# Two graph layers on one core: r transposed in 32x32 blocks through memory, W2 a graph later, row statistics on ScalarE, and the attention's result ahead of the next logits' maximum

## The reference, cut to what matters

```
# layer 0: attention with 8 heads of 64 units
feats  = h @ W[head];  e_self = feats @ a_self;  e_neigh = feats @ a_neigh
att    = softmax(leaky_relu(e_self[i] + e_neigh[j], 0.2) masked by adj)
x      = x + relu(att @ feats + b)
# layer 1: two hypergraph convolutions (H = adj != 0, w = first row of adj)
conv(v, W, b) = Dn * (H @ (Be * (H^T @ (v @ W^T)))) + b
r      = relu(conv(h, W1, b1))                    # 128 x 1024
y      = conv(layer_norm(r) * gamma + beta, W2, b2)
out    = y + h + x
```

## Time and profile before

| | |
|---|---|
| median of 3 runs | 2591.59 us |
| profiled execution, its own time | 2593.87 us |
| its span (first to last instruction) | 2591.9 us |
| TensorE busy | 2527.3 us, 98% |
| VectorE busy | 1968.6 us, 76% |
| GpSimd busy | 1630.6 us, 63% |
| ScalarE busy | 1423.3 us, 55% |
| mean granted TensorE clock | 0.993 of full speed |
| DMA queue of SyncE | 105456 packets, 201.60 MB |

### The profile page before, as it was taken

How to read it: one execution, slowest core, us unless ns; L and a number is a source line. 1 busy time by engine, 2 the same in 40 slices (tenths; PEclk the granted TensorE clock), 3 DMA queues, 4 the chain that set the end, 5 groups by cost and what they waited for, 6 DMA issues and landing times.

```text
span 2591.9 us, 50876 instructions
## 1 busy us (share of the span) xinstructions
PE 2527.3 (98%) x14996; PEld 2195.1 (85%) x14996; DVE 1968.6 (76%) x4640; ACT 1423.3 (55%) x3465; POOL 1630.6 (63%) x2068
## 2 busy tenths in 40 slices
PE   3899999999999999999999999999999999999998
PEld 2788888888888888888888888888888888888886
DVE  5877777777777777777777777777777777777774
ACT  2555555555555555555555555555555555555553
POOL 4666666666666666666666666666666666666663
PEclk8899999999999999999999999999999999999999
DMA  5122222222222222222222222222222222222210
GB/s 183 63 75 80 77 76 80 74 79 77 73 79 74 80 79 74 80 76 77 77 73 79 74 80 79 74 80 79 74 80 72 82 79 71 79 75 80 79 65 26
DMA packets 105480, 201.89 MB, mean 78 GB/s; under 512 B 20080, under 2 KB 36464, under 8 KB 105456
## 3 DMA queue, kind: packets, MB, share of 16 engines
q1 hardware_dynamic: 105456, 201.60, 23.5%
HBM read 167.39 MB, written 34.15 MB: 78 GB/s over the span
## 4 chain that ended last, share of the span: by engine, by line
PE 85%; DVE 8%; issue 3%; POOL 2%; DMA 1%; ACT 1%; SPq 0%; POOLq 0%; DVEq 0%
PE p_w1a L843 12%; PE p_w1a L839 12%; PE p_w1a L838 12%; PE p_att L917 7%; PE p_w1b L953 5%; PE p_w1b L839 5%; PE p_w1b L843 5%; PE p_w1b L838 5%; PE p_att L897 4%; PE p_fa L834 2%; PE p_fa L832 2%; PE p_fa L833 2%; PE p_fb L832 2%; PE p_fb L833 2%; PE p_fb L834 2%
## 5 line engine op out<-in xcount | busy, mean ns | idle before, releaser
L392 POOL TENSOR_TENSOR rs<-ve,halfpow 128x1 f32<-128x1 f32 x128 | 117.8, 921 | 544.8 <-DVE ve L774 544.8
L380 POOL TENSOR_TENSOR u<-u,mask 128x1024 f32<-128x1024 f32 x128 | 306.3, 2393 | 182.0 <-DMA u<-en_rows 182.0
L838 PE MATMUL p_w1a<-W_hi,rT_hi 128*128 128x512 f32 x1024 | 415.5, 406 | 0.0
L457 ACT ACTIVATE att<-u,shifts 128x128 f32<-128x128 f32 x1024 | 400.5, 391 | 18.4 <-DVE shifts L734 10.5
L839 PE MATMUL p_w1a<-W_lo,rT_hi 128*128 128x512 f32 x1024 | 404.1, 395 | 0.0
L458 ACT ACTIVATE att_low<-u,shifts 128x128 f32<-128x128 f32 x1024 | 399.5, 390 | 0.0
L843 PE MATMUL p_w1a<-W_hi,rT_lo 128*128 128x512 f32 x1024 | 280.8, 396 | 0.0
L502 ACT ACTIVATE rT_hi<-p_tb 128x512 fp32r<-128x512 f32 x128 | 76.6, 598 | 333.5 <-PE p_tb L864 333.5
L917 PE MATMUL p_att<-feats,attT 128*128 128x65 f32 x2048 | 242.9, 272 | 2.2 <-ACT attT L492 2.2
L917 PEld LDWEIGHTS p_att<-feats,attT 128*128 128x128 f32 x2048 | 239.6, 192 | 2.7 <-ACT attT L492 2.7
L789 DVE SCALAR_TENSOR_TENSOR raw<-p_w1a,rs,t_bc 128x512 f32<-128x512 f32 x128 | 96.1, 750 | 187.2 <-PE p_w1a L843 187.2
(11 more groups left out here) (125 smaller groups left out, 7216.9 us busy)
## 6 DMA issues: line engine op xcount, KB each, us to landing
u<-en_rows SPq DMA_DIRECT2D x130, 576.0 KB, 3.6
x_in<-in_x SPq DMA_DIRECT2D x128, 256.0 KB, 2.6
xT_in<-in_xT SPq DMA_DIRECT2D x128, 256.0 KB, 3.2
out<-raw SPq DMA_DIRECT2D x128, 256.0 KB, 2.0
adj_in<-in_adj SPq DMA_DIRECT2D x128, 128.0 KB, 2.5
en_rows<-eT SPq DMA_DIRECT2D x520, 1.1 KB
raw<-in_W1T SPq DMA_DIRECT2D x2, 1024.0 KB, 8.1
raw<-in_W2T SPq DMA_DIRECT2D x2, 1024.0 KB, 9.7
```

The source lines that it names most:

```text
L380: nc.gpsimd.tensor_tensor(u[:, g.slot(2), 0:HEADS, :], u[:, g.slot(2), 0:HEADS, :], mask[:, :].unsqueeze(1).broadcast_to([P, HEADS, N]), A ...
L392: nc.gpsimd.tensor_tensor(rs1[:, :], ve1[:, :], halfpow[:, :], ALU.pow).then_inc(s_rs1, 1)
L457: nc.scalar.activation(att[:, i, :], u[:, g.slot(2), i, :], ACT.Exp, bias=shifts[:, 0, i:i + 1])
L838: mm(dst, hi, w_hi, start=first, stop=False)
```

## The change

r's transposition leaves TensorE. VectorE transposes r (128 x 1024) within 32x32 blocks into rB, SyncE writes rB to a scratch in memory (`r_blocks`) and, once it has landed, reads it back by four DMAs that put the blocks in their places in rT, in runs of 32 values (128 bytes). ScalarE then makes rT_hi at the end of its turn in one instruction, VectorE rT_lo at the beginning of the next turn in one instruction.

The product with W2 is that of graph t-1, and z and y and the output are one graph later with it. There is one turn more (t up to 129). `rest` has four buffers in place of two, `rs2` two columns in place of one.

The two `bn_stats` and the `bn_aggr` over r are gone from VectorE. The two ReLUs on ScalarE also sum their rows (`accum_out`), two small instructions make the negative mean, one `Square` over 1024 columns sums the squared deviations, and another small one makes the variance; GpSimd keeps the root alone.

On ScalarE the first ReLU of r stands ahead of h0's high part, and z's high part ahead of hg's. On VectorE sizes, counts and reciprocals stand ahead of r's second half; and the maximum of the logits of t+2 with what follows it stands behind x1's statistics of t+1. The load of x of t+5 is issued by ScalarE, that of adj at the beginning of SyncE's turn.

```diff
 # turns
-    loops = (total - AHEAD - 2) // UNROLL
-    for t in range(-AHEAD, 1):
+    loops = (total - AHEAD - 3) // UNROLL
+    for t in range(-AHEAD, 2):
...
 # SyncE
+                if t.plus(5).within(NG) and (t.loop is not None or t.base >= -1):
+                    load_adj(t.plus(5))
...
-                g = t.plus(5)
-                if g.within(NG) and (g.loop is not None or g.base >= 4):
-                    load(g)
+                g = t
+                if g.within(NG):
+                    sp.wait_ge(s_rB, g.count())
+                    sp.dma_start(r_blocks[:, :], rB).then_inc(s_rB_out, 16)
+                    sp.wait_ge(s_rB_out, g.count(per=16))
+                    for c in range(4):
+                        sp.dma_start(rT[32 * c:32 * (c + 1), :].rearrange("a (k q b) -> a k q b", q=4, b=32),
+                                     r_blocks.rearrange("(q a) (k c b) -> c a k q b", q=4, c=4, b=32)[c]).then_inc(s_rT, 16)
...
 # ScalarE, in the order of its turn
                     exps(t.plus(1), 1)
+                nc.scalar.activation(r[:, 0:HALF], r[:, 0:HALF], ACT.Relu, accum_out=sum2[:, 0:1]).then_inc(s_r, 1)
                 ... h0's high part
-                ... ReLU of r's first half, rT_hi's first half
+                nc.scalar.activation(nm2a[:, :], sum2[:, 0:1], ACT.Copy, scale=-1.0 / DH).then_inc(s_nm2a, 1)
                 act.wait_ge(s_pre, g.count(per=2))
+                nc.scalar.activation(r[:, HALF:DH], r[:, HALF:DH], ACT.Relu, accum_out=sum2[:, 1:2]).then_inc(s_r, 1)
                 ... copy of the transposed attention weights of t+1
-                ... rT_hi's second half
+                nc.scalar.activation(nm2[:, :], sum2[:, 1:2], ACT.Identity, bias=nm2a[:, :], scale=-1.0 / DH).then_inc(s_nm2, 1)
+                nc.scalar.activation(dev, r, ACT.Square, bias=nm2[:, :], accum_out=sq2[:, :]).then_inc(s_sq2, 1)
                 ... G's high part (of t-1)
+                nc.scalar.activation(ve2[:, :], sq2[:, :], ACT.Identity, bias=eps[:, :], scale=1.0 / DH).then_inc(s_ve2, 1)
                     exps(t.plus(2), 0)
+                    act.wait_ge(s_x1, g.count(4))
+                    act.dma_start(x_in[:, g.slot(4), :], x[bass.ds(n, 1), :, :].rearrange("a p d -> p (a d)")).then_inc(s_in[g.slot(4)], 16)
                 ... h of t+1
+                ... z's high part of t-1, ahead of hg's high part
                 ... hg's high part of t+1
+                    act.wait_ge(s_rT, g.count(per=64))
+                    nc.scalar.activation(rT_hi[:, :], rT, ACT.Copy).then_inc(s_rT_hi, 1)
                 ... copy of G of t+2
...
 # VectorE, in the order of its turn
                     feats_of(g, 1, scale)
+                g = t.plus(-1)
+                    dve.wait_ge(s_rT_hi, g.count())
+                    nc.vector.tensor_tensor(rT_lo[:, :], rT, rT_hi[:, :], ALU.subtract).then_inc(s_rT_lo, 1)
                 ... r's first half, larger(t+1, 1), h0's low part, incidence of t+2
+                ... sizes, counts, reciprocals of t+2
                 ... r's second half
-                ... sizes, bn_stats
                 ... y (of t-2)
-                ... rT_lo's first half, bn_stats, counts, reciprocals, bn_aggr
-                ... maximum of the logits of t+2, neg_s, neg_m, shifts
+                    dve.wait_ge(s_r, g.count(per=2))
+                    nc.vector.transpose(rB, r[:, :]).then_inc(s_rB, 1)
                 ... rden, o_sc of t+1
-                ... rT_lo's second half
                 ... x1, bn_stats, inv, bn_aggr, ve1, nm1 of t+1
+                ... maximum of the logits of t+2, neg_s, neg_m, shifts
+                        dve.wait_ge(s_rs1, t.plus(1).count())
                     larger(t.plus(2), 0)
                 ... z (of t-1), statistics of t+5, hg's low part
...
 # TensorE
-                    transposes(p_ta, r[:, 0:HALF], s_rT)
-                    transposes(p_tb, r[:, HALF:DH], s_rT)
                 ... the last product is that of t-2, the product with W2 that of t-1
+                    pe.wait_ge(s_rT_hi, g.count())
+                    if t.within(NG):
+                        pe.wait_ge(s_pre, t.count(per=2) - 1)
+                    for c in range(HC):
+                        high(p_w1a[:, :], rT_hi[:, part(c)], W2_hi[:, c, :], W2_lo[:, c, :], c == 0)
+                    pe.wait_ge(s_rT_lo, g.count())
+                    for c in range(HC):
+                        last = low(p_w1a[:, :], rT_lo[:, part(c)], W2_hi[:, c, :], c == HC - 1)
```

More of the change, by code:

```diff
@@ L58, in turns @@
     with eng.Fori(0, loops) as k:
[L59 removed]
+        for u in range(2, UNROLL + 2):
             turn(Graph(u, k))
[L61 removed]
+    for t in range(2 + loops * UNROLL, total + 2):
         turn(Graph(t))
@@ L520, in turn @@
                         rounded(3)
+                g = t.plus(-1)
+                if g.within(NG):
+                    act.wait_ge(s_z, g.count())
+                    if g.has(1):
+                        act.wait_ge(s_y, g.count(1))
+                    nc.scalar.activation(z_hi[:, :], z[:, :], ACT.Copy).then_inc(s_z_hi, 1)
                 g = t.plus(1)
@@ L736, in turn @@
+                g = t
+                if g.within(NG):
+                    dve.wait_ge(s_r, g.count(per=2))
+                    if g.has(1):
+                        dve.wait_ge(s_rB_out, g.count(1, per=16))
+                    nc.vector.transpose(rB, r[:, :]).then_inc(s_rB, 1)
+                if t.base == -1:
+                    rest_of(2)
+                if t.base == -2:
+                    rest_of(1)
+                g = t.plus(2)
                 g = t.plus(1)
@@ L746, in turn @@
                                             ALU.mult).then_inc(s_osc, 1)
-                if t.within(NG):
-                    dve.wait_ge(s_rT_hi, t.count(per=2))
-                    nc.vector.tensor_tensor(rT_lo[:, HALF:DH], p_tb[:, :], rT_hi[:, HALF:DH],
-                                            ALU.subtract).then_inc(s_rT_lo, 1)
                 if g.within(NG):
@@ L921, in turn @@
                     spread()
-                g = t
+                g = t.plus(-1)
                 if g.within(NG):
-                    pe.wait_ge(s_r, g.count(per=2))
-                    if g.has(1):
-                        pe.wait_ge(s_y_sb, g.count(1))
-                    if g.plus(1).within(NG):
-                        pe.wait_ge(s_G_sb, g.plus(1).count())
-                    transposes(p_tb, r[:, HALF:DH], s_rT)
-                    for m in range(2):
-                        if g.base == 0:
-                            pe.wait_ge(k_lo2, 1 + m)
-                        pe.wait_ge(s_rT_hi, g.count(per=2) - 1 + m)
-                        for c in range(m * CB, (m + 1) * CB):
-                            high(p_w1a[:, :], rT_hi[:, part(c)], W2_hi[:, c, :], W2_lo[:, c, :], c == 0)
-                        pe.wait_ge(s_rT_lo, g.count(per=2) - 1 + m)
-                        for c in range(m * CB, (m + 1) * CB):
-                            last = low(p_w1a[:, :], rT_lo[:, part(c)], W2_hi[:, c, :], c == HC - 1)
+                    pe.wait_ge(s_rT_hi, g.count())
+                    if t.within(NG):
+                        pe.wait_ge(s_pre, t.count(per=2) - 1)
+                    for c in range(HC):
+                        if g.base == 0 and c % CB == 0:
+                            pe.wait_ge(k_lo2, 1 + c // CB)
+                        high(p_w1a[:, :], rT_hi[:, part(c)], W2_hi[:, c, :], W2_lo[:, c, :], c == 0)
+                    pe.wait_ge(s_rT_lo, g.count())
+                    for c in range(HC):
+                        last = low(p_w1a[:, :], rT_lo[:, part(c)], W2_hi[:, c, :], c == HC - 1)
                     last.then_inc(s_w2, 1)
@@ L969, in turn @@
                         pe.wait_ge(s_G_sb, g.count(1))
+                    if g.has(4):
+                        pe.wait_ge(s_y_sb, g.count(4))
                     mm(p_G, inc[:, g.slot(2), 1, :], beT[:, :], start=True, stop=True).then_inc(s_G, 1)
```

186 lines of the change are left out of this document (91 added, 95 removed).

## The result

The changed kernel takes 3074.91 us (median of 4 runs, 3065.77 to 3100.26), the kernel before 2590.73 beside it: a ratio of 1.188, with an interval of 1.184 to 1.193. It is 484 us slower. The forecast was 2920 us with a range of 2780 to 3100. The profiled execution took 3100.26 us, the longest of the four, its span 3098.3, at a mean granted clock of 0.916; the kernel before had 0.993.

The account below looks back on a forecast made before the run. TensorE's own work was taken to bound the 19.51 us turn. Turn 18.63 + 0.82 + 2.19 + 0.47 = 22.11 us, 325 us over 125 turns; 2593.87 + 325 + 11 - 10 = 2920 us, range 2780 to 3100.

Parts of the forecast that it names:

- third case: Rival: r's way through memory decides the turn; at 40 ns a packet the ring takes 25.6 us, 3357 us in all; chance 0.14.
- The product of h for h: TensorE waits for h, queued on ScalarE behind exponentials that wait for the late shifts: 8.16 - 5.97 = 2.19 us a turn.
- The attention's product for attT: TensorE waits for ScalarE's copy of the transposed attention weights, behind r's late second half and its ReLU: 0.82 us a turn.
- second case: Rival: only h is late, VectorE getting r's second half out in time; turn 21.02 us, 2784 us in all; chance 0.10.
- The restarts: TensorE's products behind the two waits take longer, 1.17 against 0.97 and 2.00 against 1.73: 0.47 us a turn.
- The clock stays: TensorE's granted clock remains 1.00 despite the waits, from a stretch with 4.31 of 5 us busy; no time added.
- 11 at the end less 10 in the first turns: 11 us more for the last graph's r through memory, 10 less because setup stalls can hide the new waits.
- The way through memory: r's write of 512 KB within 3.6 us, reads with landing 7.4, over before ScalarE comes to rT_hi: costs nothing.
- the end of like size: Lower of two prices for the reads' 128-byte packets, 21 ns against 92, from packets of the same size: 5.4 us.
- the ring: Way through memory, then rT_hi, copy of G and exponentials, to the next turn's ReLU: 20.8 us, less than the forecast turn.
- Hidden costs: VectorE's block transposition and rT_lo, some 1.2 us each, and ScalarE's statistics fit into idle time; rT_lo up to 0.3 short.
- Case 4: Rival: faster, the transposes' removal from TensorE worth 0.88 x 125 = 110 us, less 11 at the end: 2495 us; chance 0.07.

Follow-up runs that it names:

- e1: Changed kernel with VectorE's maximum of the next logits, up to the shifts, put back ahead of the attention's result: 2599.95 us, ratio 1.003 to the kernel before.
- e6: Kernel before the change with only VectorE's maximum of the logits of t+2, up to the shifts, moved behind x1's statistics of t+1: 3080.37 us, ratio 1.188.
- e10: Changed kernel, maximum still late, with exps(t+2, 0) moved from ahead of h to ScalarE's turn end and larger(t+2, 0) a turn later: 3262.48 us, ratio 1.257.
- e4: Changed kernel with unread TensorE products added, 3 ahead of the wait for attT and 8 ahead of the wait for h: 2881.39 us, ratio 1.111.
- e7: e1 with r's blocks read from memory twice, by four more DMAs, and rT_hi waiting for all eight: 3075.5 us, ratio 1.187 to the kernel before.
- e5: e1 with two parts of the features of t+3 moved on TensorE to ahead of the attention's product: 2601.43 us, ratio 1.003 to the kernel before.
- e2: Changed kernel with r's second half ahead of sizes and counts on VectorE, h0's high part ahead of r's first ReLU on ScalarE: 2874.05 us, ratio 1.108.
- e8: e1 with h0's high part put back ahead of r's first ReLU on ScalarE: 2566.22 us, ratio 0.990 to the kernel before.

## Why the prediction was right, and where it was not

**The time.** The measured 3074.91 us lie above the forecast's own range, 2814 to 3029. They lie within the stated range only because its upper end was widened for the mild part of the third case, the way through memory, which had no part in it. That the range holds is luck; that the kernel became slower, and by which two waits, is not.

**The product of h for h: right, by its steps.** In the turn from 1074.78 the way runs as worked out. Changed kernel, VectorE, then ScalarE:

```profile
1076.81 0.21 DVE L768 RECIPROCAL rden<-p_att 128x8 f32<-128x8 f32 x1 [1.64 <-PE p_att L952]
1079.76 1.21 DVE L803 TENSOR_REDUCE neg_max<-u 128x8 f32<-128x1024 f32 x1
1081.42 0.17 DVE L812 TENSOR_TENSOR shifts<-e_blk,neg_m 128x16 f32<-128x16 f32 x1
```

```profile
1081.71 0.40 ACT L474 ACTIVATE att<-u,shifts 128x128 f32<-128x128 f32 x1 [5.15 <-DVE shifts L812]
1082.07 0.34 ACTq L549 DMA_DIRECT2D x_in<-in_x  x1
...
1084.06 0.80 ACT L558 ACTIVATE h<-x,nb,rs 128x512 f32<-128x512 f32 x1
```

From the product's end (1074.78 + 2.00) to the product of h (1084.99) it is 8.21 us; 8.16 were forecast, and the wait was 2.17 where 2.19 stood. The load of x on ScalarE goes out between exponentials and costs nothing; 0.10 had been taken. e1 takes the cause away and the wait goes, e6 makes it alone and the wait comes, e10 moves the exponentials alone and the wait goes.

**The attention's product for attT: there, but of two kinds.** Forecast 0.82 us. In most turns shown it is 0.26 to 0.57, because the counts take 0.17 and not the 0.39 of the earlier trace rows, and a row sum adds about 0.10 to a ReLU in place of 0.14. In the others it is 2.0 to 2.5: there the counts last 1.9 to 2.4 us beside GpSimd's addition, in 32 of 129 executions, or the incidence 2.5, in three. Together 0.96 a turn; that this is near 0.82 is luck. The had the sign of it: 0.39 us for two columns is long, and the prediction saw that (in its second case) but took it only as something that could shrink.

**The restarts: right where the clock held.** The products behind the two waits take 1.15 and 2.00 us, as in the earlier trace rows.

**"The clock stays": the step that failed.** It was put at nothing, from a single row of the last turns at 4.31 of 5 us busy and 1.00. The runs showed that in the changed kernel, behind a single wait of 2.0 to 2.5 us, the clock mostly falls to 0.50 for some microseconds, and e4 that it stays when the waits are filled. That row, with 0.69 us idle in all, held no wait of that length. The price stands in the window of the main part, 122 turns:

```profile
135.82:3008.56 2872.74, 2537.95 (x13298) 2180.84 (x13299) 1978.05 (x4025) 1544.26 (x4027) 1552.90 (x1828) 0.92 0.39 109
```

TensorE is busy 2537.95 / 122 = 20.80 us a turn, against 19.14 in the turn at full clock: 1.66 us a turn, 203 us in 122 turns. With this term the sum closes: 18.63 + 0.96 + 1.85 + 0.47 + 1.66 = 23.57 us a turn, against 2872.74 / 122 = 23.55 measured; 125 x (23.57 - 19.51) = 508 us, against 3100.26 - 2593.87 = 506 in the two profiled executions. The forecast's 11 at the end less 10 in the first turns was not tried.

**The way through memory: rightly given no part in this kernel, but for a reason that is half luck.** The write lands in 2.6 us (at most 3.6 forecast), and the four reads go out in 2.8 to 2.9 and land 2.9 behind their issue, some 5 together where 7.4 were taken: the packets cost no more than the end of like size. In the turn from 1074.78 the write is issued at 1075.20, so all has landed by about 1075.2 + 2.6 + 5 = 1082.8, and rT_hi starts at 1086.67. It waited for the reads once, 2.8 us in all. By the Trainium skill's "VectorE: DVE Perf Modes", section "The three transpose paths", a plain DMA that transposes by strides is slow, 19 times slower than the DMA's own transposition, where the innermost stride is large. With runs of 128 bytes the reads took some 5 us; no run here shows the unblocked case or the DMA's own transposition. But the ring's forecast of 20.8 us was above the 18.63 that the transposes' removal promised, and e7 shows what that meant: once the other waits are gone, this way is at its limit.

**Hidden costs.** The block transposition takes 1.25 us (1.2 forecast) and delays nothing that the chain needs. rT_lo was put at 1.2 us within 1.47 of idle time; it takes 1.67 in the mean, and in the turn from 1074.78 r's first half starts right behind it with no idle time left (in 51 of 128 turns VectorE still waits there, 40.4 us in all). It stands in the ring that is read from e5's turn.

**The cases.** Case 2 (only h late) was made by e2: 2874 us, not 2784: its turns at full clock last 21.09 us where 21.02 were forecast, and the clock makes the rest. Case 4 (faster) was at 2495 us; e1 and e8 show that even without a late h the turn is 19.3 us, not 18.6: 2600 and 2566 us. Its price had counted TensorE's own work as the only bound; the steps of e5 say that another path is about as long as the old turn of 19.51 us, which no edit has confirmed.

## What to carry to other kernels

An instruction moved on one in-order engine moves all that is queued behind its consumers: the maximum gave way to eight instructions, 2.95 us in all (1076.81 to 1079.76), which wait for the attention's product, and through ScalarE's queue it held h, which had hardly any room. Price a new wait of some microseconds on TensorE with the clock it loses behind it, not by its own length; here the clock was 40% of the loss (203 of the 506 us between the profiled executions). And work taken off the bound is worth only the distance to the next path: work that ring out before counting the gain.

## What the runs showed of the hardware

A granted clock of 0.50 for some microseconds behind one wait of 2.1 to 2.5 us in an otherwise full turn; not behind each one (at 1084.99 it stayed, and in e2, with waits of some 2.3 us for h alone, it stayed in 76 of 121 turns, for a reason that was not found), and hardly at all where products that nobody reads filled the wait (0.992). An instruction of VectorE over 128x2 that starts beside a GpSimd addition over 128x1024 may take 2.2 to 2.4 us, ending with it, in place of 0.17; a VectorE subtraction of two tiles of 128x1024 (rT_lo) takes 1.21 to 2.34 us by what GpSimd does beside it. The one that begins second is the longer one: at 219.16 us it began 0.07 us behind GpSimd's xc (128x512) and took 2.33, xc 1.31; at 478.70 it began 0.07 us ahead of xc and took 1.22, xc 2.31. That GpSimd is the cause is read from the records' times and from e8, in which the counts keep out of its way; it was not tried with GpSimd's addition taken out. 512 KB read in runs of 128 bytes by four DMAs lands within some 5 us of the first issue.
